# Two centring instructions of VectorE change their place in a graph layer with a residual norm

## The chip, the cores and the metric

The kernel runs on one core of a Trainium2 chip. The metric is the time of one execution on the device in microseconds (us), lower is better; the time before is the median of three runs. Engines are called as in the profile: PE (TensorE), DVE (VectorE), ACT (ScalarE), POOL (GpSimd), SP (SyncE, which only issues DMAs here).

## The reference

`x` has 50,000 rows (nodes) of 64 numbers; there are 25,000 edges with `src`, `dst` (sorted), a type out of 10 and 64 attributes.

```
t_r = x[src] @ W[type];  h_r = x[dst] @ W[type]
att = sum(t_r * tanh(h_r + edge_attr))
a   = softmax of att over the edges of one dst
h   = sum over the edges of one dst of x[src] * a
out = leaky((x + h) @ W1.T) + leaky((x * h) @ W2.T)
y   = layernorm(x + out)
```

Nodes without an edge have h = 0; for them, and at first for all, only the dense part x + leaky(x @ W1.T) and its norm count.

## The kernel before, in words

**Dense part.** The 50,000 rows are 49 dense tiles of 1024 rows (128 partitions x 8 rows of 64 numbers = 128 x 512). Each is loaded by SP, transposed and multiplied by PE, then on DVE added (`dense_add`, L974), summed per row (`dense_total`, L979), centred (`dense_centre`, L984: row sum x -1/64 + row, all in SBUF); ACT squares it (`dense_square`, L684); DVE sums the squares (`dense_sum`, L989); ACT takes the root (L730), DVE its inverse (L996), ACT scales each row (`dense_norm`, L691) and SP stores it (L311).

**Edge part.** The edges lie as 128 partitions x 196 columns; a block is 8 columns, 25 blocks. POOL gathers the rows of x for both ends of a column by an indirect DMA (L441), 384 in all; some columns are fetched row by row by SP (L377). DVE multiplies the transposed rows by ten type masks (`mask(s, 0..9)`, L912, reading PSUM), PE multiplies with the ten weights, ACT takes tanh, DVE the product (L919). One step later come the scores: the running maximum (`score_max`, L928), `differences` (L936, L937), `restarts` (L942), ACT's exponentials and weighting, and eight running sums `sum_one` (L954, 128 x 64). Two steps later the ending block: `pair` (L1004, L1005: h + x and h * x), PE's products, `leaky` (L1011), `final_add` (L1016), `final_add_x` (L1021). Three steps later, for block l: `final_sum` (L1026), `final_centre` (L1032), ACT's `final_square` (L736), `final_squares` (L1039), and ACT's `final_out` (L743). POOL then scatters the finished rows column by column over the dense result by an indirect DMA (L465), 196 in all.

**Order.** Each engine has its own queue, written out by hand as a loop over steps s = -1 to 28. In step s DVE handles masks of block s, scores and sums of e = s - 1, the ending of f = s - 2, the norm of l = s - 3, and dense tiles D0, D1, D2 = 3s+3, 3s+4, 3s+5; DP = 3s + 2 is the last dense tile of the step before. Dense tiles end with step 15. Engines wait on semaphores only; an instruction that follows one of its own engine waits only where a semaphore is named.

POOL's whole work is one queue: all gathers, then a wait for all dense stores, then all scatters. Before most of them it waits for a mark of PE's progress (`pace`), before a block's gathers for a free buffer (13 deep), before a block's scatters for ACT's scaled rows:

```
for s in range(NS):
    gather(s)
for k in range(RO):
    pool.wait_ge(o_stored[k], o_need(k))
...
def scatter(s):
    pool.wait_ge(fmul_done, s + 1)
    for j in range(cols(s)):
        pace(G_MOVES[NS] + c, s)
        pool.indirect_dma_start(...)
```

The last issue of POOL (L482) is a single row block for groups of edges that cross partitions.

Of the kernel before, what the change touches and what calls it, by code (L numbers as in the profile page):

```python
# [34 lines left out]
def wait(eng, sem, value):  # L35

    if value > 0:
        eng.wait_ge(sem, value)


def gnn_resnorm(nc, x, src, dst, eattr, etype, relw, resw, resw2, out):
# [14 lines left out]
    def cols(s):  # L56
        return min(COLS, T - s * COLS)

    def groups(s):
        return cols(s) // QUAD  # L60
# [7 lines left out]
    def tiles(s):  # L68
        return [d for d in range(3 * s + 3, 3 * s + 6) if 0 <= d < ND]
# [26 lines left out]
    with ExitStack() as ctx:  # L96
# [317 lines left out]
        def _(pool):  # L414
# [12 lines left out]
            def pace(n, scattered_blocks):  # L427
                step_end = ends[min(NS - 1, RW + 4 + scattered_blocks)]
                need = [k for k, (_, _, work) in enumerate(marks) if work <= min(n * PACE - LEAD if n < G_MOVES[NS] else n * PACE_OUT - LEAD_OUT, step_end)]
                if need and need[-1] > at[0]:  # L430
                    at[0] = need[-1]
                    pool.wait_ge(marks[at[0]][0], marks[at[0]][1])
# [395 lines left out]
        def _(v):  # L828
# [77 lines left out]
            def mask(s, r):  # L906
                n = cols(s) * P
                if r == 0:
                    v.wait_ge(xT_done, s + 1)
                    v.wait_ge(typ_in[s % RT], turn(s, RT) * DMA)  # L910
                wait(v, quad_done, s * R + r + 1 - RM)
                v.scalar_tensor_tensor(xm[:, (s * R + r) % RM, 0:n], typ[:, s % RT, 0:n], float(r), xT_ps[:, 0:n],  # L912
                                       ALU.is_equal, ALU.mult).then_inc(masked, 1)
# [7 lines left out]
            def score_max(e):  # L921
                c, n = e * COLS, cols(e)
                b = (e % 2) * COLS
                v.wait_ge(att_done, e + 1)
                if e == 0:
                    v.wait_ge(setup_d, 3)
                wait(v, max_done, e)
                v.tensor_tensor_scan(m_all[:, c + 1:c + 1 + n], start[:, c:c + n], s_ps[:, b:b + n],  # L928
                                     m_all[:, c:c + 1], ALU.add, ALU.max).then_inc(max_done, 1)
# [14 lines left out]
            def sum_one(e, j):  # L944
                if j >= cols(e):
                    return
                c = e * COLS + j
                v.wait_ge(wx_done, G_BEFORE[e] + j // QUAD + 1)
                wait(v, chain_done, c)
                if j == 0 and e >= RS:  # L950
                    v.wait_ge(h_done, G_BEFORE[e - RS + 1])
                    v.wait_ge(hist_stored[e % RS], e // RS * DMA)
                old = es[:, e % RS, j - 1, :] if j else es[:, (e - 1) % RS, COLS - 1, :]
                v.scalar_tensor_tensor(es[:, e % RS, j, :], old, wd[:, e % 2, 1, j:j + 1], wx[:, j, :],  # L954
                                       ALU.mult, ALU.add).then_inc(chain_done, 1)
# [25 lines left out]
            def dense_centre(d):  # L981
                v.wait_ge(zsum_done, d + 1)
                z = zd[:, d % RZ, :].rearrange("p (j f) -> p j f", f=D)
                v.scalar_tensor_tensor(z, zsd[:, :].unsqueeze(2).to_broadcast([P, DR, D]), -1.0 / D, z, ALU.mult, ALU.add).then_inc(zmid_done, 1)  # L984
# [13 lines left out]
            def pair(f):  # L998
                n = cols(f)
                xd = xsd[:, f % RX, 0:n, 1, :]  # L1000
                v.wait_ge(h_done, G_BEFORE[f + 1])
                if f > 0:
                    v.wait_ge(tr_in, TR_PAIR[f - 1, groups(f - 1) - 1] + 1)
                v.tensor_tensor(uw[:, 0:n, 0, :], h_t[:, 0:n, :], xd, ALU.add)  # L1004
                v.tensor_tensor(uw[:, 0:n, 1, :], h_t[:, 0:n, :], xd, ALU.mult).then_inc(uw_done, 1)  # L1005
# [22 lines left out]
            def final_centre(f):  # L1028
                n = cols(f)
                v.wait_ge(fsum_done, f + 1)  # L1030
                wait(v, fmul_done, f - 1)
                v.scalar_tensor_tensor(zcf[:, f % 2, 0:n, :], zs[:, 0:n].unsqueeze(2).to_broadcast([P, n, D]), -1.0 / D,  # L1032
                                       zf[:, 0:n, :], ALU.mult, ALU.add).then_inc(fsub_done, 1)
# [8 lines left out]
            for s in range(-1, LAST + 1):  # L1042
                main, e, f, l = 0 <= s < NS, s - 1, s - 2, s - 3
                D0, D1, D2 = (n if n in tiles(s) else None for n in (3 * s + 3, 3 * s + 4, 3 * s + 5))
                DP = 3 * s + 2 if 3 * s + 2 in tiles(s - 1) else None
                on, ending, late = 0 <= e < NS, 0 <= f < NS, 0 <= l < NS
# [7 lines left out]
                    mask(s, 1)  # L1054
                if on:
                    score_max(e)
                if DP is not None:
                    dense_centre(DP)
                if main:
                    mask(s, 2)  # L1060
                if on:
# [4 lines left out]
                    restarts(e)  # L1066
                if ending:
                    pair(f)
                if main:
                    mask(s, 4)  # L1070
                if main:
# [25 lines left out]
                    mask(s, 8)  # L1097
                if D0 is not None:
                    dense_centre(D0)
                if on:  # L1100
                    sum_one(e, 6)
                    sum_one(e, 7)
                if late:
                    final_centre(l)
                if main:
                    mask(s, 9)
                if D1 is not None:
# [105 lines left out]
```

## Time and profile before

| what | us |
|---|---|
| median of three runs (772.3 to 774.19) | 772.67 |
| the profiled execution | 767.71 |
| its span, first to last instruction | 765.7 |
| POOL's gathers (L441), 384 | 377.8 busy |
| POOL's scatters (L465), 196 | 201.6 busy |
| DVE busy | 634.9 |

Busy time is the time in which an engine had an instruction of the program in work. In a timeline a row is start, duration, engine, line, operation, output and inputs, shapes, count; instructions of one line that follow each other are merged into one row. Idle time of the engine ahead of an instruction stands in brackets, with what ended it; "issue" means that no wait shows. Consecutive DVE instructions overlap a little in the records: each starts some 0.08 us before the end of the one ahead.

### The profile page before, as it was taken

To read this page: it belongs to the slowest core of one execution; us is meant where nothing else is said; L and a number is where in the kernel's file an instruction comes from. 1 tells how busy PE (TensorE), PEld (TensorE's weight loads), DVE (VectorE), ACT (ScalarE), POOL (GpSimd) and SP (SyncE) were. 2 spreads that over 40 slices of the span, in tenths; PEclk is the share of its full clock that TensorE was granted. 3 is DMA by queue.
4 is the path that set the end of the run, shared out by engine and by line. 5 is a ranking of instruction groups with operands and counts; after the bars stand their busy time and mean duration, and the time that the engine had idled before them with its cause. 6 is when DMAs were issued, how large, how long until landed. Compare 5 with 4: busy or idle time off the path is not lost. (4 is left out here: it accounts for less than half of the span.)

```text
span 765.7 us, 14665 instructions
## 1 busy us (share of the span) xinstructions
PE 552.6 (72%) x3780; PEld 291.9 (38%) x3780; DVE 634.9 (83%) x1115; ACT 498.1 (65%) x1474; POOL 582.5 (76%) x590
## 2 busy tenths in 40 slices
PE   1887888888788788788888887888888778532000
PEld 0552454445345345345345343433333333321000
DVE  1689999999999999999999999999999989742010
ACT  0366768679779779779779777765665446755040
POOL 6777777777777777777777777777777777777776
PEclk9999999999999999999999999999999989855555
DMA  5463434434434434433433332322112221000000
GB/s 132 111 185 82 124 98 134 123 83 151 123 91 140 125 98 133 128 109 120 137 107 111 107 107 69 107 73 74 37 56 73 73 79 48 30 26 17 19 18 16
DMA packets 49457, 70.41 MB, mean 92 GB/s; under 512 B 17450, under 2 KB 20966, under 8 KB 49374
## 3 DMA queue, kind: packets, MB, share of 16 engines
q1 hardware_dynamic: 30750, 52.33, 21.1%
q0 software_dynamic: 18624, 17.16, 10.5%
q8 instruction: 30, 0.49, 0.3%
q14 instruction: 53, 0.43, 0.2%
HBM read 45.61 MB, written 25.78 MB: 93 GB/s over the span
## 5 line engine op out<-in xcount | busy, mean ns | idle before, releaser
L441 POOL DMA_INDIRECT xsd<-in_x,ends_i x384 | 377.8, 984 | 117.9 <-issue 110.7
L543 PE MATMUL t_ps<-xm,w_rel 64*64 64x512 f32 (+1 forms) x1000 | 269.4, 620 | 38.3 <-DVE xm L912 35.6
L912 DVE SCALAR_TENSOR_TENSOR xm<-typ,xT_ps 128x1024 f32<-128x1024 f32 (+1 forms) x250 | 291.8, 1184 | 2.7 <-issue 2.7
L545 PE MATMUL h_ps<-xm,w_rel 64*64 64x512 f32 (+1 forms) x1000 | 269.4, 620 | 0.0
L465 POOL DMA_INDIRECT out<-out_r,row_i x196 | 201.6, 1029 | 60.0 <-issue 57.2
L560 PE MATMUL y_ps<-bd_cat,dT 128*128 128x256 f32 x392 | 97.9, 394 | 19.7 <-DVE zd L974 17.5
L691 ACT ACTIVATE o_t<-zd,rstd 128x64 f32<-128x64 f32 x392 | 98.8, 339 | 15.3 <-DVE rstd L996 15.3
L543 PEld LDWEIGHTS t_ps<-xm,w_rel 64*64 64x64 f32 x1000 | 52.7, 134 | 142.0 <-DVE xm L912 107.0
L578 PE MATMUL s_ps<-bd_both,uwT 128*128 128x128 f32 x392 | 72.6, 310 | 39.9 <-issue 39.1
L578 PEld LDWEIGHTS s_ps<-bd_both,uwT 128*128 128x128 f32 x392 | 54.3, 200 | 115.9 <-issue 96.1
L560 PEld LDWEIGHTS y_ps<-bd_cat,dT 128*128 128x128 f32 x392 | 72.7, 195 | 33.1 <-issue 14.6
L698 ACT ACTIVATE wd<-delta 128x16 f32<-128x16 f32 (+1 forms) x25 | 5.4, 216 | 97.2 <-DVE delta L942 55.4
L954 DVE SCALAR_TENSOR_TENSOR es<-es,wd,wx 128x64 f32<-128x64 f32 x196 | 55.3, 282 | 11.6 <-ACT wx L704 0.6
L568 PE MATMUL tr_ps<-ident,uw 128*128 128x128 f32 x196 | 32.9, 292 | 27.5 <-ACT uwT L718 15.5
L545 PEld LDWEIGHTS h_ps<-xm,w_rel 64*64 64x64 f32 x1000 | 52.7, 134 | 0.0
L704 ACT ACTIVATE wx<-xsd,wd 128x64 f32<-128x64 f32 x196 | 52.1, 337 | 0.8
L723 ACT COPY l<-s_ps 128x256 f32<-128x256 f32 x98 | 35.3, 360 | 24.1 <-PE s_ps L578 24.1
L711 ACT ACTIVATE h_t<-es,rs 128x64 f32<-128x64 f32 x196 | 49.4, 337 | 0.0
L743 ACT ACTIVATE out_r<-zcf,rstd 128x64 f32<-128x64 f32 x196 | 49.1, 333 | 0.1
L568 PEld LDWEIGHTS tr_ps<-ident,uw 128*128 128x128 f32 x196 | 21.4, 145 | 67.2 <-issue 36.0
L974 DVE TENSOR_TENSOR zd<-rd,y_ps 128x512 f32<-128x512 f32 x49 | 33.3, 679 | 9.6 <-ACT rd L677 9.0
L736 ACT ACTIVATE sqf<-zcf 128x512 f32<-128x512 f32 (+1 forms) x25 | 15.6, 622 | 34.4 <-DVE zcf L1032 33.6
(143 smaller groups left out, 753.8 us busy)
## 6 DMA issues: line engine op xcount, KB each, us to landing
xsd<-in_x SPq DMA_DIRECT2D x1024, 0.2 KB
x_in<-in_x SPq DMA_DIRECT2D x48, 256.0 KB
typ<-typ_d SPq DMA_DIRECT2D x24, 512.0 KB
out<-o_t SPq DMA_DIRECT2D x48, 256.0 KB
xsd<-in_x,ends_i POOLq DMA_INDIRECT x384
hist<-es SPq DMA_DIRECT2D x24, 256.0 KB, 2.0
ea<-in_edge_attr SPq DMA_DIRECT2D x24, 224.0 KB
out<-out_r,row_i POOLq DMA_INDIRECT x196, 2.2
```

Of the source, the lines that this page charges most:

```text
L441: pool.indirect_dma_start(xsd[:, s % RX, j, side, :], None, x[:, :], bass.IndirectOffsetOnAxis(ap=ends_i[:, side, c:c + 1], axis=0),).then ...
L465: pool.indirect_dma_start(out[:, :], bass.IndirectOffsetOnAxis(ap=row_i[:, c:c + 1], axis=0), out_r[:, s % RW, j, :], None, bounds_check=t ...
L543: pe.matmul(t_ps[h * D:(h + 1) * D, 0:n], w_rel[0:D, r, :], xm[0:D, b, h * n:(h + 1) * n], start=(r == 0), stop=(r == R - 1), skip_group_c ...
L545: mm = pe.matmul(h_ps[(1 - h) * D:(2 - h) * D, 0:n], w_rel[D:P, r, :], xm[D:P, b, (1 - h) * n:(2 - h) * n], start=False, stop=(r == R - 1) ...
L560: mm = pe.matmul(y_ps[:, j * 2 * P:(j + 1) * 2 * P], dT[:, d % 2, j * P:(j + 1) * P], bd_cat.rearrange("p k f -> p (k f)"), start=True, st ...
L568: mm = pe.transpose(tr_ps[:, j * P:(j + 1) * P], uw[:, g * QUAD + j, :, :].rearrange("p k f -> p (k f)"), ident[:, :])
L578: mm = pe.matmul(s_ps[:, YQ + j * P:YQ + (j + 1) * P], uwT[:, q // 2, k * P:(k + 1) * P], bd_both[:, :], start=True, stop=True)
L691: ins = act.activation(o_t[:, d % RO, j * D:(j + 1) * D], zd[:, d % RZ, j * D:(j + 1) * D], ACT.Copy, scale=rstd[:, s % 2, d % 3, j:j + 1])
L704: ins = act.activation(wx[:, j, :], xsd[:, e % RX, j, 0, :], ACT.Copy, scale=wd[:, e % 2, 0, j:j + 1])
L711: ins = act.activation(h_t[:, j, :], es[:, f % RS, j, :], ACT.Copy, scale=rs[:, f % 2, j:j + 1])
L912: v.scalar_tensor_tensor(xm[:, (s * R + r) % RM, 0:n], typ[:, s % RT, 0:n], float(r), xT_ps[:, 0:n], ALU.is_equal, ALU.mult).then_inc(mask ...
L954: v.scalar_tensor_tensor(es[:, e % RS, j, :], old, wd[:, e % 2, 1, j:j + 1], wx[:, j, :], ALU.mult, ALU.add).then_inc(chain_done, 1)
```

## The change

DVE's queue is reordered at two places; no instruction is added, removed or altered, and the other engines' queues are the same. In a step the centring of tile DP stood behind `score_max` and ahead of mask 2; it now stands behind `pair` (L1004, L1005) and ahead of mask 4. `final_centre` of block l stood behind `sum_one` 6 and 7 and ahead of mask 9; it now stands behind the centring of D0 and ahead of sums 6 and 7.

```
                 if on:
                     score_max(e)
-                if DP is not None:
-                    dense_centre(DP)
                 if main:
                     mask(s, 2)
...
                     restarts(e)
                 if ending:
                     pair(f)
+                if DP is not None:
+                    dense_centre(DP)
                 if main:
                     mask(s, 4)
...
                     mask(s, 8)
                 if D0 is not None:
                     dense_centre(D0)
+                if late:
+                    final_centre(l)
                 if on:
                     sum_one(e, 6)
                     sum_one(e, 7)
-                if late:
-                    final_centre(l)
                 if main:
                     mask(s, 9)
```

## Rows read from the trace of the kernel before

**Rows 1.** The page: busy us of each engine, share of the span, instructions.

```profile
PE 552.6 (72%) x3780; PEld 291.9 (38%) x3780; DVE 634.9 (83%) x1115; ACT 498.1 (65%) x1474; POOL 582.5 (76%) x590
```

**Rows 2.** POOL's waits: us in total, times, longest us.

```profile
POOL xsd L441 <- issue: 110.7, 363, 0.3
```

**Rows 3.** Groups of POOL's instructions: busy us, mean ns | idle before.

```profile
L441 POOL DMA_INDIRECT xsd<-in_x,ends_i x384 | 377.8, 984 | 117.9 <-issue 110.7 <-PE h_ps L545 2.7 <-PE s_ps L578 1.5
L465 POOL DMA_INDIRECT out<-out_r,row_i x196 | 201.6, 1029 | 60.0 <-issue 57.2 <-PE h_ps L545 1.8 <-PE s_ps L578 0.6
```

**Rows 4.** Timeline of POOL, last block and last issue.

```profile
756.21 0.97 POOL L465 DMA_INDIRECT out<-out_r,row_i  x1 [0.30 <-issue]
...
761.32 0.97 POOL L482 DMA_INDIRECT out<-out_fix,fix_i  x1 [0.30 <-issue]
```

**Rows 5.** Timeline of ACT, the last finished rows.

```profile
737.25 1.05 ACT L743 ACTIVATE out_r<-zcf,rstd 128x64 f32<-128x64 f32 x4
```

**Rows 6.** Timeline of POOL in the gather phase.

```profile
303.01 1.24 POOL L441 DMA_INDIRECT xsd<-in_x,ends_i  x1 [0.30 <-issue]
...
313.31 1.46 POOL L441 DMA_INDIRECT xsd<-in_x,ends_i  x1 [0.30 <-issue]
...
325.06 0.94 POOL L441 DMA_INDIRECT xsd<-in_x,ends_i  x1 [0.30 <-issue]
...
479.76 2.04 POOL L441 DMA_INDIRECT xsd<-in_x,ends_i  x1 [0.30 <-issue]
```

**Rows 7.** Timeline of DVE over the same stretch.

```profile
302.26 1.17 DVE L1011 SCALAR_TENSOR_TENSOR l<-l 128x1024 f32<-128x1024 f32 x1
...
307.78 2.34 DVE L912 SCALAR_TENSOR_TENSOR xm<-typ,xT_ps 128x1024 f32<-128x1024 f32 x2
...
310.18 0.68 DVE L984 SCALAR_TENSOR_TENSOR zd<-zsd,zd 128x512 f32<-128x512 f32 x1
...
313.27 0.68 DVE L1004 TENSOR_TENSOR uw<-h_t,xsd 128x512 f32<-128x512 f32 x1
313.87 0.68 DVE L1005 TENSOR_TENSOR uw<-h_t,xsd 128x512 f32<-128x512 f32 x1
...
324.49 0.68 DVE L984 SCALAR_TENSOR_TENSOR zd<-zsd,zd 128x512 f32<-128x512 f32 x1
325.08 0.68 DVE L954 SCALAR_TENSOR_TENSOR es<-es,wd,wx 128x64 f32<-128x64 f32 x2
...
336.09 2.34 DVE L912 SCALAR_TENSOR_TENSOR xm<-typ,xT_ps 128x1024 f32<-128x1024 f32 x2
...
479.70 0.68 DVE L1004 TENSOR_TENSOR uw<-h_t,xsd 128x512 f32<-128x512 f32 x1
```

**Rows 8.** Timeline of ACT: its square of the step's tile DP.

```profile
314.60 0.61 ACT L684 ACTIVATE sqd<-zd 128x512 f32<-128x512 f32 x1
```

**Rows 9.** Timeline of POOL in the scatter phase.

```profile
511.56 1.46 POOL L465 DMA_INDIRECT out<-out_r,row_i  x1 [0.30 <-issue]
...
517.15 1.50 POOL L465 DMA_INDIRECT out<-out_r,row_i  x1 [0.30 <-issue]
...
536.00 1.87 POOL L465 DMA_INDIRECT out<-out_r,row_i  x1 [0.31 <-issue]
```

**Rows 10.** Timeline of DVE in the scatter phase.

```profile
510.90 0.66 DVE L954 SCALAR_TENSOR_TENSOR es<-es,wd,wx 128x64 f32<-128x64 f32 x2
511.48 0.69 DVE L1032 SCALAR_TENSOR_TENSOR zcf<-zs,zf 128x512 f32<-128x512 f32 x1
...
514.64 1.22 DVE L1011 SCALAR_TENSOR_TENSOR l<-l 128x1024 f32<-128x1024 f32 x1 [0.37 <-ACT l L723]
...
517.12 0.67 DVE L1021 TENSOR_TENSOR zf<-zf,xsd 128x512 f32<-128x512 f32 x1
```

**Rows 11.** Timeline of POOL: the first scatter.

```profile
498.65 1.00 POOL L465 DMA_INDIRECT out<-out_r,row_i  x1 [0.54 <-issue]
```

**Rows 12.** Timeline of SP: the last dense tile's store.

```profile
495.25 0.73 SPq L311 DMA_DIRECT2D out<-o_t  x2
```

More of the change, by code:

```diff
@@ L1056, in _ @@
                     score_max(e)
-                if DP is not None:
-                    dense_centre(DP)
                 if main:
@@ L1068, in _ @@
                     pair(f)
+                if DP is not None:
+                    dense_centre(DP)
                 if main:
@@ L1099, in _ @@
                     dense_centre(D0)
+                if late:
+                    final_centre(l)
                 if on:
@@ L1102, in _ @@
                     sum_one(e, 7)
-                if late:
-                    final_centre(l)
                 if main:
```

## The prediction

> **What bounds the kernel now.** I read the busy times first. DVE is busy for 83% of the span, POOL for 76%, PE for 72% [rows 1], so the share alone points at DVE. It misleads here. The second view is POOL's waits: POOL's idle time before its 580 indirect DMAs is nearly all "issue", 0.3 us at most before a gather [rows 2] and the same before scatters but for one 0.54 us [rows 11]. An engine that never waits is the bound. The groups of POOL's instructions give the sum: 384 gathers of 984 ns and 117.9 us between them, 196 scatters of 1029 ns and 60.0 us between them [rows 3]: 377.8 + 117.9 + 201.6 + 60.0 = 757.3 us. The last issue ends at 761.32 + 0.97 = 762.3 us [rows 4]; the 5.0 us that the sum lacks are the setup ahead of the first gather and two single issues. What follows is the last landing, to 765.7 us. The data are ready long before: the last finished rows are scaled at 737.25 to 738.3 us and their first scatter starts at 756.21 us [rows 4, 5], 17.9 us later. No other engine has work on the output after that.
>
> So an edit of DVE's order counts only by what it does to POOL. There are two ways: DVE's marks come so late that POOL must wait, or DVE slows POOL's issues.
>
> The second way is visible. Most gathers last 0.94 us, but in every step one lasts 1.24 and one 1.46 us [rows 6]. Lay DVE's timeline beside them [rows 7]. The gather at 303.01 starts inside L1011 (302.26 to 303.43) and ends at 304.25, 0.82 us behind L1011's end. The one at 313.31 starts 0.04 us after L1004 did (313.27 to 313.95) and ends at 314.77, again 0.82 us behind. The scatter at 511.56 starts inside L1032 (511.48 to 512.17), lasts 1.46 in place of 0.97, and ends 0.85 us behind it; the one at 517.15 does the same with L1021 [rows 9, 10]. I call such an issue caught. What catches is a long DVE instruction with two SBUF inputs: L984, L1004, L1005, L1011, L1016, L1021, L1032. The ten masks of a step (one input in PSUM) and L954 (64 columns) catch nothing. An issue that starts less than 0.13 us before the DVE instruction's end, or just before its start, goes free: the gather at 325.06 starts inside L984's last 0.11 us and lasts 0.94 [rows 6, 7].
>
> This also ties POOL to DVE while dense tiles last. A DVE step takes 336.09 - 307.78 = 28.31 us [rows 7]; POOL makes 22 issues in it, 22 x 1.25 = 27.5 us free, and the two catches (0.30 + 0.51 = 0.81 us) fill the rest. A POOL that ran ahead would be caught longer, and so held to DVE's step. The pattern stands from about 142 to 455 us, eleven times.
>
> **Part one: the last dense tile's centring (L984) goes from behind the running maximum to behind the pair, in steps 0 to 15.** Nothing is added or removed: one DVE instruction of 0.68 us, with the next one starting 0.60 us behind its start (as from 313.27 to 313.87), changes place [rows 7]. Masks 2 and 3, the differences and the pair come 0.60 us earlier, mask 4 and all behind it stay. Who waits? ACT squares that tile at 314.60 [rows 8]; in the new order the centring ends at about 313.87 + 0.68 = 314.55, so the square moves by nothing. If that cover went, ACT's queue behind it (the eight scalings of finished rows, then the pair's copy) would slip by up to the 0.6 us moved. The earlier restarts and pair can only help ACT's weights and PE. The square's sum on DVE comes two masks later, over 2 us. Cost on DVE: 0.
>
> For POOL, the slot from 313.87 to 314.55 that was L1005's is now L984's, the slot that was L1004's (313.27) is L1005's, and L1004 lies one slot earlier, where no issue starts (the gather before starts 1.25 us ahead of 313.31, at 312.06, the new L1004 at 312.67). So the same gather is caught by an instruction of the same length: 0. The old place of L984 (310.18) caught nothing in these steps, so nothing is gained there.
>
> The Trainium skill speaks against this part: its page "SBUF — State Buffer", section "SBUF: two separate sides", says that DVE and GpSimd share a port pair as an exclusive lock, against a GpSimd operation that reads SBUF whenever DVE has two SBUF inputs, and that the loser blocks fully. By that rule three such instructions in a row are a longer barrier than two; the rows agree that the loser blocks, and what it makes of the time is the third rival.
>
> **Part two: centring of finished rows (L1032) goes ahead of running sums 6 and 7, in steps 3 to 27.** Again one instruction of 0.60 us moves. Sums 6 and 7 come 0.60 us later; behind them are the store of the history on SP (its buffer comes round only four steps later) and the normaliser, whose place is behind mask 9 and stays. ACT's square of these rows may start earlier, but in the dense steps ACT is busy with the tile's own square until then; in the later steps pair outputs bound by PE decide, so DVE's step does not shorten. Cost on DVE: 0; bounds 0.2 us either way per run.
>
> In the gather phase the new L1032 starts at about 325.08, a few hundredths from the gather at 325.06. A catch needs DVE to be first by about 0.03 us (the narrowest seen is L1021's 517.12 against 517.15). I take: not caught. If caught, it costs 0.68 - 0.13 = 0.55 us once, not per step, since POOL then meets L1016 and the new L984 in place of L1011 and L1005, with again some 0.8 us per step.
>
> In the scatter phase the move has an effect. At 511.56 the old L1032 caught a scatter for 0.48 us; the new one occupies 510.90 to 511.58 [rows 10], and that scatter goes free. The same stands twice more (about 554 and 596 us): 3 x 0.48 = 1.44 us. Further on: the issues come 0.48 us earlier, one starts at 515.39 inside L1011 (514.64 to 515.86) and is caught for 0.34, the next at 517.01 is ahead of L1021's 517.12 and is spared 0.52. Sum of the first passage: -0.48 + 0.34 - 0.52 = -0.66 us. Two DVE steps on, the shift also turns the long catch at 536.00 (1.87 us, 0.90 over [rows 9]) into one of 0.3. Three passages together give at most -3 us. But after about 610 us the masks thin out and the catches are irregular; the longest, L1011 at full length, costs 1.22 - 0.12 = 1.1 us. An issue stream shifted by 1 to 3 us meets other instructions there, and with starts laid against the rows two catches take 1.8 us back. I take -1.2 us; the ends are -3.0 and, if more is taken back than was gained, +1.5.
>
> **Sum** against the profiled execution: 0 + 0 - 1.2, so a span of 764.5 us, from 765.7. Its own time, 767.71, lies 5.0 us below the median of the three runs, 772.67; I carry the difference over: 772.67 - 1.2 = 771.5 us. What can be told from no change is 0.3%, 2.3 us.
>
> **Rivals.**
> (a) Much more is gained in the scatter phase: all three passages hold and nothing is taken back, -3.0 us, 769.7. For it: the three passages are alike to 0.01 us. Against: L1021 caught by 0.03 us only, so in other runs that catch may not exist, and the gain neither.
> (b) POOL is caught by the new L1032 once, and the scatter phase falls badly: +0.6 + 1.5 = +2.1, 774.8.
> (c) Slower: the longer barrier. At 479.76 a gather was caught by L1004 (479.70) and held through L1005 as well: 2.04 us, 1.10 over [rows 6, 7]. With three in a row such a gather would be held some 0.6 us more. If that became the rule, the 0.30 at L1011 would vanish but 0.3 us per step stay, over 14 steps +4.2 us: 776.9. It decides from 0.16 us per step. Against: of the steady steps not one shows it; POOL gets in between two DVE instructions nearly always.
> (d) DVE's dense step itself changes by some 0.1 us, as ACT or PE get their work sooner; POOL is tied to that step, so 15 x 0.1 = 1.5 us either way: 770.0 to 773.0 together with the forecast, still within 0.3% or at its edge.
> (e) The first scatter waits for the last dense tile's store, issued at 495.25 [rows 12], 2.9 us ahead of the last gather's end at 498.11; the scatter's idle time is 0.54 in place of 0.30 us [rows 11]. SP is busy issuing single rows before it, so the edit moves it little: up to 0.5 us if late.
>
> **Chances.** The forecast with (d) and (e), within 0.3%: 0.68. (a) and its like, faster by over 2.3 us: 0.20. (c), and the worst of (b): 0.12. The range reaches to (a) and to (b): 769.3 to 774.7.
>
> **What would show it.** POOL idle before issues still at most 0.3 us; DVE's step in the dense phase still 28.31 us; the gather phase ends near 498.1 us, with L1005 in L1004's place as the catcher at 0.5 us; no scatter caught by L1032 between 500 and 610 us; ACT's square of the last dense tile unmoved. The prediction is wrong if gathers of 1.5 us appear at L1032, if issues of 2 us appear at the pair, or if POOL shows waits on PE's marks.

## The result and the profile after

The changed kernel takes 766.85 us (median of 4 runs, 766.31 to 767.59) against 772.88 us before (4 runs): ratio 0.992, 95% interval 0.9893 to 0.9947, so 6.0 us or 0.8% faster. The forecast was 771.5 us, within 0.3%; the range ended at 769.3. On a second chip the ratio was 0.9955 (0.9936 to 0.9974), 3.8 us.

The profiled execution of the changed kernel has a span of 764.9 us, only 0.8 us less than the 765.7 of before. One profile of each kernel therefore doesn't carry the explanation; the experiments below do.

What the two profiles do give is the time by phase. POOL's 85th and last scatters, before and then after:

```profile
612.67 0.97 POOL L465 DMA_INDIRECT out<-out_r,row_i  x1 [0.30 <-issue]
...
760.04 0.97 POOL L465 DMA_INDIRECT out<-out_r,row_i  x1 [0.31 <-issue]
```

```profile
609.72 0.97 POOL L465 DMA_INDIRECT out<-out_r,row_i  x1 [0.30 <-PE h_ps L545]
...
759.15 0.97 POOL L465 DMA_INDIRECT out<-out_r,row_i  x1 [0.30 <-issue]
```

The last gather ends at 498.11 us before and at 498.53 after. The first 84 scatters (from the first one's start to the 85th's) take 114.0 us before and 110.9 after; the other 112, to the end of the last, take 148.3 and 150.4. So in this pair the scatter phase gains 3.1 us and gives 2.1 back, close to the 3.0 and 1.8 of the prediction, and the gather phase is no shorter.

POOL's waits and groups after, in the columns of [rows 2, 3]:

```profile
POOL xsd L441 <- issue: 108.6, 356, 0.3
...
POOL out L465 <- issue: 55.5, 182, 0.3
```

```profile
L441 POOL DMA_INDIRECT xsd<-in_x,ends_i x384 | 378.2, 985 | 118.0 <-issue 108.6 <-PE h_ps L545 5.5 <-PE y_ps L560 1.2
L465 POOL DMA_INDIRECT out<-out_r,row_i x196 | 200.6, 1023 | 59.7 <-issue 55.5 <-PE h_ps L545 3.4 <-PE s_ps L578 0.9
```

POOL is still the engine that hardly ever waits: 378.2 + 118.0 + 200.6 + 59.7 = 756.5 us of its own work and issue time.

DVE's timeline in the dense phase, and POOL's beside it (for [rows 7] and [rows 6]):

```profile
278.92 1.21 DVE L912 SCALAR_TENSOR_TENSOR xm<-typ,xT_ps 128x1024 f32<-128x1024 f32 x1
...
307.11 2.34 DVE L912 SCALAR_TENSOR_TENSOR xm<-typ,xT_ps 128x1024 f32<-128x1024 f32 x2
...
311.99 0.69 DVE L1004 TENSOR_TENSOR uw<-h_t,xsd 128x512 f32<-128x512 f32 x1
312.59 0.69 DVE L1005 TENSOR_TENSOR uw<-h_t,xsd 128x512 f32<-128x512 f32 x1
313.19 0.69 DVE L984 SCALAR_TENSOR_TENSOR zd<-zsd,zd 128x512 f32<-128x512 f32 x1
...
324.41 0.71 DVE L1032 SCALAR_TENSOR_TENSOR zcf<-zs,zf 128x512 f32<-128x512 f32 x1
```

```profile
312.63 1.47 POOL L441 DMA_INDIRECT xsd<-in_x,ends_i  x1 [0.30 <-issue]
...
324.39 0.95 POOL L441 DMA_INDIRECT xsd<-in_x,ends_i  x1 [0.30 <-issue]
```

The catcher of the long gather is now L1005: it starts 0.04 us ahead of the gather at 312.63, which lasts 0.52 us too long, as L1004 did before. The new L1032 starts 0.02 us behind the gather at 324.39 and catches nothing. But the step is 307.11 - 278.92 = 28.19 us, where it was 28.31.

Three of this profile's dense steps are longer again, by 0.35 us each. In them DVE waits at L919, the product that needs ACT's tanh (L667):

```profile
331.95 0.69 DVE L919 TENSOR_TENSOR prod<-t_ps,g_t 128x512 f32<-128x512 f32 x1 [0.26 <-ACT g_t L667]
```

The other profile of the changed kernel has three such waits as well, that of part one alone has two of 0.12 and 0.17 us, and no profile of a kernel without part one has any. What makes ACT late there is not shown.

ACT's timeline at the two squares. First after, then before (rows that were not shown ahead of the prediction):

```profile
313.92 0.63 ACT L684 ACTIVATE sqd<-zd 128x512 f32<-128x512 f32 x1 [0.49 <-DVE zd L984]
...
325.03 0.63 ACT L684 ACTIVATE sqd<-zd 128x512 f32<-128x512 f32 x1
325.56 0.62 ACT L736 ACTIVATE sqf<-zcf 128x512 f32<-128x512 f32 x1
326.08 0.58 ACT L677 ACTIVATE rd<-y_ps 128x512 f32<-128x512 f32 x1
```

```profile
325.70 0.63 ACT L684 ACTIVATE sqd<-zd 128x512 f32<-128x512 f32 x1
326.39 0.63 ACT L736 ACTIVATE sqf<-zcf 128x512 f32<-128x512 f32 x1
326.93 0.58 ACT L677 ACTIVATE rd<-y_ps 128x512 f32<-128x512 f32 x1
```

The square of DP lies 313.92 - 307.11 = 6.81 us into the step; before it was 314.60 - 307.78 = 6.82. It didn't move. At the other place, from L684's start to L677's it is 1.23 us before and 1.05 after. Before, ACT waited there for the final centring for a few hundredths of a microsecond, and the relu (L677) came late for DVE's add of tile D1.

POOL's timeline in the scatter phase after (for [rows 9, 11]):

```profile
498.83 1.00 POOL L465 DMA_INDIRECT out<-out_r,row_i  x1 [0.30 <-issue]
...
510.71 0.97 POOL L465 DMA_INDIRECT out<-out_r,row_i  x1 [0.30 <-issue]
...
514.54 1.34 POOL L465 DMA_INDIRECT out<-out_r,row_i  x1 [0.30 <-PE h_ps L545]
516.18 0.97 POOL L465 DMA_INDIRECT out<-out_r,row_i  x1 [0.30 <-issue]
```

In this phase no scatter is caught by L1032; the one at 514.54 is caught by L1011 for 0.36 us, and L1021 is passed.

### The profile page after: what moved, and what is told of

The parts are those of the page before. It is cut to its first block and busy times, and to the rows that moved or that the text cites. A ratio compares the mean times of both kernels' runs of the same rounds, so it can differ in the third digit from the quotient of the medians.

```text
span 764.9 us, 14665 instructions
## 1 busy us (share of the span) xinstructions
PE 556.2 (73%) x3780; PEld 293.9 (38%) x3780; DVE 634.8 (83%) x1115; ACT 499.1 (65%) x1474; POOL 581.8 (76%) x590
## 5 line engine op out<-in xcount | busy, mean ns | idle before, releaser
L441 POOL DMA_INDIRECT xsd<-in_x,ends_i x384 | 378.2, 985 | 118.0 <-issue 108.6
L465 POOL DMA_INDIRECT out<-out_r,row_i x196 | 200.6, 1023 | 59.7 <-issue 55.5
L954 DVE SCALAR_TENSOR_TENSOR es<-es,wd,wx 128x64 f32<-128x64 f32 x196 | 55.7, 284 | 11.7 <-ACT wx L704 0.6
L684 ACT ACTIVATE sqd<-zd 128x512 f32<-128x512 f32 x49 | 30.9, 631 | 12.7 <-DVE zd L984 12.6
```

The source lines that it names most:

```text
L441: pool.indirect_dma_start(xsd[:, s % RX, j, side, :], None, x[:, :], bass.IndirectOffsetOnAxis(ap=ends_i[:, side, c:c + 1], axis=0),).then ...
L465: pool.indirect_dma_start(out[:, :], bass.IndirectOffsetOnAxis(ap=row_i[:, c:c + 1], axis=0), out_r[:, s % RW, j, :], None, bounds_check=t ...
```

## The experiments

In each, the ratio is to runs of the kernel before on the same chip. It is not exactly the quotient of the two medians, so microseconds by the ratio and by the medians can differ by up to 1 us. The chips differ: the kernel before has medians of 767.4 (first four kernels), 769.4 (second four) and 768.2 us (third four), so only ratios are compared between them.

### The kernel before against itself

> The kernel before, unchanged, timed against itself. Theory 1 (catches on POOL's issues: which issues are caught depends on how the issue stream lies against DVE's instructions, and the kernel before can lie in more than one way): ratio 1.000 and a time of 772 to 774 us, while its profiled execution may fall at 767 to 768 or at 772 to 774 us; in the latter POOL shows 5 us more time in its issues than the 25.8 us above their free lengths (0.946 us a gather, 0.975 us a scatter) that the profile of before shows, and still no idle time over 0.55 us. Theory 2 (POOL waits in those executions for PE's marks): a slow execution would show POOL idle for more than 0.5 us at some issues, in sum 5 us.

Measured: ratio 0.9984 (0.9974 to 0.9994), 766.5 us; runs of 765.65 to 769.62. The interval leaves out 1 though the kernels are identical, so a difference under 0.2% means little. Its profiled execution, 769.62 us, is the longest of its ten, with this first scatter:

```profile
500.46 1.00 POOL L465 DMA_INDIRECT out<-out_r,row_i  x1 [1.75 <-DMA out<-o_t]
```

DVE's first mask started at 33.64 us in it, at 31.82 in the profile of before, and this delay reached the end: POOL waited for the last dense tile's store. Theory 1's claim, that a longer execution has more time in the issues, is hardly what this one shows: above the free lengths of 0.946 and 0.975 us the gathers and scatters have 25.9 us, in the profile of before 25.0 (not the 25.8 of the expectation). Theory 2's claim, idle time at PE's marks, doesn't appear at all. The 2.1 us by which its span is longer are mostly that late start. The 772 to 774 us of the first chip did not come back on it.

### Each part alone, and both

```
# part one alone
-                if DP is not None:
-                    dense_centre(DP)      (behind score_max)
+                if DP is not None:
+                    dense_centre(DP)      (behind pair)
# part two alone
+                if late:
+                    final_centre(l)
                 if on:
                     sum_one(e, 6)
                     sum_one(e, 7)
-                if late:
-                    final_centre(l)
```

> Part one alone: DP's centring behind the pair, final centring where it was. Theory 1a (the gain of 6 us is made in the dense phase, where part one works on all 16 steps): 766 to 768 us, -5 to -7. Theory 1b (the gain is made by the final centring's new place): 772 to 774 us, no change. My prediction's sum said 0 for this part.

> Part two alone: the final centring ahead of running sums 6 and 7, DP's centring where it was. Theory 1a: 771 to 773 us, 0 to -1.5. Theory 1b: 766 to 768 us, -5 to -7. My prediction's sum said -1.2 for this part.

> Both parts, the changed kernel again on the same chip as its parts: 766 to 768 us by either theory; if it comes out at 772 to 774 here, the difference is between chips and not between kernels.

| kernel | median us | ratio | 95% interval |
|---|---|---|---|
| part one | 766.88 | 0.9993 | 0.9974 to 1.0013 |
| part two | 763.68 | 0.9946 | 0.9924 to 0.9968 |
| both | 763.57 | 0.9955 | 0.9936 to 0.9974 |

The whole gain is part two's. Part one gives nothing that can be told from zero, as the sum had it; its interval spans 3 us. The size is 0.45 to 0.54% here, less than on the first chip.

### Part two by phase, and the last dense store

```
# dense steps only: the new place if s <= 15, else the old one
+                if late and s <= 15:
+                    final_centre(l)
                 (sums 6 and 7)
+                if late and s > 15:
+                    final_centre(l)
# late steps only: the two conditions exchanged
# store: in SP's queue
+                if s == 16:
+                    for n in tiles(s - 1)[0:2]:
+                        store_o(n)
                 rows_at((s - 1) * PER_STEP + 2)
                 (the stores behind it, now only if s is not 16)
```

> Part two in steps 3 to 15 only. Theory L (the last dense tile's store sets when the scatters begin: in the three profiles without part two the first scatter starts 0.90 us behind the store's landing, and part two shortens DVE's dense step from 28.31 to 28.19 us, so that store comes earlier): -1.5 to -2.5 us against before, and the first scatter not later than 0.55 us behind the last gather. Theory C (fewer issues caught by L1032 in the scatter phase): no change, within 0.5 us.

> Part two in steps 16 to 27 only. Theory L: no change, within 0.5 us; DVE's dense step stays 28.31 us. Theory C: -1.3 to -3 us, with under 1 us of POOL's scatters caught by L1032 in place of 2.1 to 3.7. Both together would give -1.5 to -2.5 here and the same at the dense steps.

> The kernel before, with one thing moved in SP's queue: in step 16 the last dense tile's store stands ahead of 16 single-row loads instead of behind them, so it is issued some 3.5 us earlier. Theory L: -0.5 to -2 us (the profiles of before and of its repeat show 0.24 and 1.45 us of wait at the first scatter beyond the usual 0.30), and the first scatter 0.3 us behind the last gather. Theory C: no change.

> Part two (all steps) with that store moved as well. Theory L: the landing is then out of the way, and what is left of part two's gain is what the gather and scatter phases give: 0 to -1 us beyond part two alone (763.7 us where before is 767.4). Theory C: the same as part two alone, within 0.5 us.

| kernel | median us | ratio | 95% interval |
|---|---|---|---|
| dense steps only | 767.47 | 0.9978 | 0.9970 to 0.9987 |
| late steps only | 765.38 | 0.9955 | 0.9942 to 0.9967 |
| store alone | 768.85 | 1.0000 | 0.9992 to 1.0009 |
| part two and store | 763.85 | 0.9930 | 0.9919 to 0.9942 |

Two gains stand beside each other: 0.22% (1.7 us) from the dense steps and 0.45% (3.5 us) from the late ones; their sum, 0.67%, is close to the 0.70% of part two and the store together. The first of them is barely above the 0.16% by which the kernel differed from itself; what supports it is DVE's shorter step. Neither theory alone was right. Theory L as to the store fell: with the store out of the way the time is the same within 0.1%. What that store can cost shows in an execution in which DVE starts late. The profile of the store alone has such a start too (first mask at 33.67 us, in the kernel against itself at 33.64), and its first scatter starts at 499.17 us where the other's waited until 500.46.

For the late steps two profiles of this batch can be laid side by side, since one of the kernels (store alone) runs like before. POOL's timeline with the centring at the old place (store alone; L469 is its scatter):

```profile
513.55 1.45 POOL L469 DMA_INDIRECT out<-out_r,row_i  x1 [0.30 <-issue]
...
519.16 1.48 POOL L469 DMA_INDIRECT out<-out_r,row_i  x1 [0.30 <-issue]
...
538.00 1.86 POOL L469 DMA_INDIRECT out<-out_r,row_i  x1 [0.31 <-issue]
```

POOL's timeline with it at the new place in the late steps, and DVE's:

```profile
511.76 0.97 POOL L465 DMA_INDIRECT out<-out_r,row_i  x1 [0.30 <-issue]
...
515.59 1.32 POOL L465 DMA_INDIRECT out<-out_r,row_i  x1 [0.30 <-issue]
517.22 0.98 POOL L465 DMA_INDIRECT out<-out_r,row_i  x1 [0.30 <-issue]
...
536.75 1.32 POOL L465 DMA_INDIRECT out<-out_r,row_i  x1 [0.30 <-issue]
```

```profile
511.10 0.68 DVE L1032 SCALAR_TENSOR_TENSOR zcf<-zs,zf 128x512 f32<-128x512 f32 x1
...
514.84 1.22 DVE L1011 SCALAR_TENSOR_TENSOR l<-l 128x1024 f32<-128x1024 f32 x1 [0.33 <-ACT l L723]
...
517.31 0.68 DVE L1021 TENSOR_TENSOR zf<-zf,xsd 128x512 f32<-128x512 f32 x1
```

At the old place the profile repeats [rows 9] to 0.02 us a catch: 0.48, 0.51, 0.89. At the new one the scatter at 511.76 starts 0.02 us before L1032's end and goes free, the one at 515.59 is caught by L1011 for 0.35, the one at 517.22 is 0.09 us ahead of L1021, and in place of 0.89 stands 0.35. That is the first passage as the prediction laid it out (0.34 at L1011, ahead of L1021), and then the second and third. The first 84 scatters take 114.43 us (499.17 to 613.60) at the old place and 110.69 (498.80 to 609.49) at the new one: -3.7 us. The 112 from there to the end take 148.25 and 148.79 us: +0.5 us back. Counted in issues, POOL makes 15 and 16 in turn in DVE's late steps of 21.15 us at the old place, and 16 in each at the new one. One issue more in every second step, 1.27 us each, is the same gain.

This pair is not the whole record. The old place has a second pattern. In the profile of "dense steps only" the late steps are those of before, and yet it shows this in every step:

```profile
509.58 1.46 POOL L465 DMA_INDIRECT out<-out_r,row_i  x1 [0.30 <-issue]
...
530.80 1.46 POOL L465 DMA_INDIRECT out<-out_r,row_i  x1 [0.30 <-issue]
```

L1032 catches a scatter each time for 0.48 us, but the catches at L1021 and the long one at L1011 are missing, POOL makes 16 issues a step, and the first 84 scatters take 111.4 us. All profiles on chips where POOL is the bound, but for two with one more instruction in the late steps, by the place of the final centring there:

| place, profiles | first 84, us | other 112, us |
|---|---|---|
| old: before, before against itself, store alone | 113.9 to 114.4 | 148.3 to 148.7 |
| old: part one | 112.3 | 148.7 |
| old: dense steps only; ACT's order (below) | 111.4; 111.6 | 147.8; 148.3 |
| old: longer dense step (below) | 112.8 | 147.4 |
| new: after, part two, both, late steps only, part two and store | 110.6 to 111.4 | 148.7 to 150.4 |

So the new place avoids the slow pattern in all five of its profiles, and the old one sometimes does so too, by how POOL happens to enter the phase. The profiles of "dense steps only" and of ACT's order are each the shortest execution of their kernel (763.33 us where the next is 766.95; 763.73 where the median is 766.59), so the fast pattern is probably not their usual one; how often an unprofiled execution falls into it is not on record. What is given back behind the 84th scatter is 0.5 us only in the pair above. Over these profiles it lies between nothing and 3 us.

### Catches by themselves

```
+                if 17 <= s <= 23:
+                    v.tensor_tensor(free buffer 128x1024, typ[...], typ[...], ALU.mult)
                 if main:
                     mask(s, 6)
# the other kernel: second input xT_ps (PSUM) in place of typ
```

> The kernel before with one more DVE instruction in each of steps 17 to 23, ahead of mask 6: a product of 128x1024 with both inputs in SBUF, written to a buffer that is free by then (its result is not used). DVE gets 7 x 1.1 = 8 us more work, which POOL's lead of 14 us and more covers. Theory C (POOL's issue is held while a long DVE instruction reads two SBUF inputs): a scatter that starts anywhere in the first 1.05 us of it is held to its end, on average 7 x 0.43 = 3 us; expected +1 to +5 us. Rival R (what counts is when DVE's work ends, or nothing): the same as the next run, within 1 us.

> The same extra product with one input in PSUM, of the same size and at the same place. Theory C: no scatter is held by it; the time moves by no more than a shift of the other catches makes, -1.5 to +1.5 us, and is clearly below the run with two SBUF inputs. Rival R: both runs move alike.

Two SBUF inputs: 771.28 us, ratio 1.0049 (1.0029 to 1.0068). One: 770.27 us, ratio 1.0027 (1.0008 to 1.0046). The two intervals overlap, so the times alone don't decide. The rows do. DVE and POOL with two SBUF inputs:

```profile
549.31 1.22 DVE L1081 TENSOR_TENSOR x_in<-typ 128x1024 f32<-128x1024 f32 x1
```

```profile
550.25 1.13 POOL L465 DMA_INDIRECT out<-out_r,row_i  x1 [0.30 <-issue]
```

and with one:

```profile
548.92 1.22 DVE L1081 TENSOR_TENSOR x_in<-typ,xT_ps 128x1024 f32<-128x1024 f32 x1
```

```profile
549.85 0.97 POOL L465 DMA_INDIRECT out<-out_r,row_i  x1 [0.30 <-issue]
```

DVE's instruction has the same length, and the scatter starts 0.94 and 0.93 us into it. With two SBUF inputs the scatter lasts 1.13 us, with one 0.97. This is so in all seven steps (1.11 to 1.13 against 0.97): DVE's instruction with two SBUF inputs holds the issue, the one with an input in PSUM doesn't. 7 x 0.15 = 1.0 us is also the difference of the medians, but that is a coincidence: in the two profiles the first 84 scatters, with five of the seven holds, take 115.13 and 115.10 us, so the holds were made good elsewhere. I had expected 3 us; POOL's issues happened to meet only the last 0.28 us of the instruction each time. That both kernels are slower than before by 2 us at least was not foreseen beyond my 1.5 us. In their profiles about that much is there before the first extra instruction (at 505.47 and 505.08 us) has run. The first scatter, with two SBUF inputs and with one, where it was 498.65 before:

```profile
500.89 1.00 POOL L465 DMA_INDIRECT out<-out_r,row_i  x1 [0.30 <-issue]
```

```profile
500.50 1.00 POOL L465 DMA_INDIRECT out<-out_r,row_i  x1 [0.30 <-issue]
```

Each has one gather in the dense phase that was held through both L1004 and L1005 (at 199.34 and 227.62 us, 2.05 us long), and from that step on POOL is one issue behind. The edit adds nothing to those steps; it acts from step 17. So the times of these two kernels say little of the extra instruction, and the rows carry the reading alone.

### What ties POOL to DVE in the dense phase, and where the 0.12 us are from

```
# longer dense step, in steps 3 to 15, ahead of mask 6
+                    v.tensor_tensor(extra[:, 0:256], typ[...0:256], xT_ps[:, 0:256], ALU.mult)
# ACT's order alone, DVE unchanged
+                if D1 is not None:
+                    dense_relu(D1)
                 if 0 <= l < NS:
                     final_square(l)
-                if D1 is not None:
-                    dense_relu(D1)
```

> The kernel before with one more short DVE instruction (128x256, one input in PSUM, result not used) in each of steps 3 to 15: DVE's dense step grows by about 0.3 us, 13 x 0.3 = 3.9 us. Theory T (POOL's gathers are tied to DVE's step by the catches): most of it appears in the time, +2.5 to +4.5 us, and the last gather ends that much later. Rival F (POOL issues at its own pace): 0 to +0.5 us.

> The kernel before with ACT's queue changed at one place and DVE's not at all: the relu of dense tile D1 goes ahead of the square of the finished rows. If part two shortened the dense step because DVE's add of D1 (L974) waited for that relu, and the relu stood behind a square that waited for the final centring, this run too has a dense step of 28.19 us or less in place of 28.31 and gains -1 to -2 us; the scatter phase is as before. If the shorter step had another cause, the step stays 28.31 us and the time the same.

The longer step: DVE's dense step becomes 337.48 - 308.86 = 28.62 us. Its first masks in two dense steps, and POOL's last gather:

```profile
308.86 2.34 DVE L913 SCALAR_TENSOR_TENSOR xm<-typ,xT_ps 128x1024 f32<-128x1024 f32 x2
...
337.48 2.34 DVE L913 SCALAR_TENSOR_TENSOR xm<-typ,xT_ps 128x1024 f32<-128x1024 f32 x2
```

```profile
501.27 0.94 POOL L442 DMA_INDIRECT xsd<-in_x,ends_i  x1 [0.30 <-issue]
```

The last gather ends at 502.2 us where it was 498.1, 4.1 us for 13 x 0.31 = 4.0 us of DVE. POOL makes 22 issues in each of these steps, as it did at 28.31 us. POOL's idle time before each issue stays 0.30: it is held in its issues alone, and tied to DVE's step. First scatter of that kernel (L466 in it), for [rows 11]:

```profile
502.51 1.00 POOL L466 DMA_INDIRECT out<-out_r,row_i  x1 [0.30 <-issue]
```

The time grew less, ratio 1.0021 (0.9998 to 1.0045), 770.06 us: the scatter phase of its profile is 2.2 us shorter than that of before. The stretch is tied; what it hands on to the next is not kept whole.

ACT's order alone: 766.59 us, ratio 0.9967 (0.9943 to 0.9991), -1.6 us by the medians and -2.5 by the ratio. ACT's timeline of it:

```profile
324.76 0.63 ACT L684 ACTIVATE sqd<-zd 128x512 f32<-128x512 f32 x1
325.29 0.58 ACT L677 ACTIVATE rd<-y_ps 128x512 f32<-128x512 f32 x1
325.76 0.62 ACT L736 ACTIVATE sqf<-zcf 128x512 f32<-128x512 f32 x1
```

DVE's dense step is 306.84 - 278.69 = 28.15 us:

```profile
278.69 2.34 DVE L912 SCALAR_TENSOR_TENSOR xm<-typ,xT_ps 128x1024 f32<-128x1024 f32 x2
...
306.84 2.34 DVE L912 SCALAR_TENSOR_TENSOR xm<-typ,xT_ps 128x1024 f32<-128x1024 f32 x2
```

With DVE's queue untouched the dense step shrinks as under part two. So the 0.12 us were the relu's lateness: DVE's add of D1 waited for it behind mask 9. The last gather of this profile ends at 496.4 us, 1.7 earlier than before. The expectation that the scatter phase is as before did not hold in it: it lies in the fast pattern (first 84 in 111.6 us), so not all of this kernel's gain need be the dense step's.

### Earlier still, and the fastest version: on chips where POOL is not the bound

```
# late steps: the centring ahead of sums 4 and 5, or behind them
+                if late and s > 15:
+                    final_centre(l)
                 if on:
                     sum_one(e, 4)
                     sum_one(e, 5)
# third kernel: part two in all steps and ACT's order as above
```

> In steps 16 to 27 only, the final centring stands ahead of sums 4 and 5 (2.5 us earlier than in the kernel before, 1.9 us earlier than in part two). Laid against the rows of before, the scatter at 509.00 would start 0.06 us inside it (508.94 to 509.6) and be held for 0.48 us, just as the one at 511.56 is in the kernel before, at every second step. Theory C (where the centring meets POOL's starts): first 84 scatters 113 to 114.5 us as in the profile of before (114.0), total within 1 us of before. Theory E (the earlier the centring, the sooner ACT, PE and DVE go on): at least the gain of part two in the late steps, -3 us or more.

> The same, but behind sums 4 and 5, ahead of the inverse roots: 0.6 us later than the run above, 1.9 us earlier than before. The scatter at 510.28 starts 0.1 us behind its end (509.5 to 510.2) and goes free. Theory C: first 84 scatters 110.5 to 111.5 us, total -2 to -4 us, as with part two in the late steps. Theory E: the same as the run above, within 0.5 us.

> Part two in all steps, with ACT's relu of D1 ahead of the square of finished rows as well: a candidate for the fastest. The dense step should be 28.15 to 28.19 us, the first 84 scatters 110.5 to 111.5 us; total -4 to -5.5 us against before. If the relu's new place adds nothing to part two, it equals part two alone (0.9946 on another chip).

> The same kernel as h1, on another chip; on the first one every kernel took 915 us with POOL waiting for over 100 us, which says nothing of catches. In steps 16 to 27 the final centring stands ahead of sums 4 and 5, where by the rows of before it meets a scatter's start at every second step. Theory C: first 84 scatters 113 to 114.5 us, total within 1 us of before. Theory E (earlier is better): -3 us or more.

> The same kernel as h2, on another chip: the centring behind sums 4 and 5. Theory C: first 84 scatters 110.5 to 111.5 us, total -2 to -4 us. Theory E: as the run above, within 0.5 us.

> The same kernel as h3, on another chip: part two in all steps and ACT's relu of D1 ahead of the square. Dense step 28.15 to 28.19 us, first 84 scatters 110.5 to 111.5 us, total -4 to -5.5 us against before.

Both times, on two chips, the kernel before itself took 915 to 916 us. The ratios: ahead of sums 4 and 5 0.9994 and 1.0006, behind them 1.0000 and 0.9987, part two with ACT's order 0.9997 and 0.9994, all with intervals that hold 1. The first of these on the second chip, POOL's waits ("remote" is a wait that the profile can't tie to an instruction of this core's queues):

```profile
POOL xsd L441 <- remote: 59.1, 41, 3.7
POOL xsd L441 <- PE h_ps L545: 27.7, 27, 1.9
...
POOL out L465 <- DMA out<-o_t: 12.6, 1, 12.6
```

The mean granted clock of TensorE is 0.845 there, 0.91 to 0.93 in the profiles on the other chips, and the dense steps take 31 to 37 us. POOL waits for marks of PE and, for 12.6 us, for the last dense store. It is likely that what a catch costs is then taken from a wait; no run was made to show it. So the question behind these runs stays open in its direct form, and whether part two with ACT's order is the fastest version wasn't measured where it could show. The lowest ratios measured are 0.992, of the changed kernel on the first chip, and 0.993, of part two with the store moved on another.

## Why the prediction was wrong

**The bound: right.** POOL's queue sets the end; it is idle 0.3 us before its issues in the profile after, and the rows show no other way for DVE's edits to act. The list of what catches has one line too many: no issue started inside L1016 in any of the fourteen profiles in which POOL is the bound, so whether it catches is not shown. The tie to DVE's step in the dense phase was right too and was shown by the longer step.

**Part one, 0: right within the noise.** Alone it gives 0.9993 (0.9974 to 1.0013). In the profile after, L1005 took L1004's place as the catcher and the square of DP lies at 6.81 us in the step against 6.82. "Cost on DVE: 0" is not quite what the rows show: the waits at L919 make DVE's thirteen dense steps 1.0 us longer with both parts (368.5 us) than with part two alone (367.5), and no time on record shows that. The barrier of rival (c) exists but is rare: in the profile after one gather of the dense steps was held from L1005 through L984.

```profile
170.77 2.07 POOL L441 DMA_INDIRECT xsd<-in_x,ends_i  x1 [0.30 <-issue]
```

It cost POOL one issue's place in that step (21 in place of 22), and POOL stayed behind. In the other profile of the same kernel, which has the waits at L919 but no such hold, the gather phase ends at 497.36 us in place of 498.53; the hold is what kept the profile after from ending it earlier than before. Part one is not needed for such a hold: the two kernels with the extra product had one each through L1004 and L1005, three such holds in the steady dense steps of fourteen profiles.

**Part two, dense steps, "Cost on DVE: 0": this step failed.** I wrote that in the dense steps ACT is busy with the tile's own square until the final centring is there. It was busy until a few hundredths before it, and behind that wait stood the relu for which DVE's add of D1 waited. The step shrank by 0.12 us, some 13 times, and POOL is tied to it. That makes 1.6 us; measured were 1.7 (0.9978), 1.6 to 2.5 us with ACT's order alone. Rival (d) had this mechanism and the price, 1.5 us, but it was counted as inside the forecast.

**Part two, late steps, "-1.2 us": the mechanism was right, this term was mis-sized.** 1.2 us was forecast and 3.5 us (0.9955) measured. Of its two sizes, the gain of the passages was put at 3.0 us at most, though the prediction's own rows add up to 0.66 + 0.60 = 1.26 us a passage and 3.8 for three; measured were 3.7 in the pair of the experiments and 3.1 in the pair of the result. The part that the irregular end takes back was put at 1.8 and measured 0.5 in the one pair and 2.1 in the other. It was the weak term: it rested on two catches, laid behind the last rows that repeat. So the pair that the forecast was worked out from came out at about its net size, -1 us in the scatter phase, and the timed runs did not: they gained some 2 us more. Which of the two patterns each execution falls into could make that difference; that is argued, not shown. Rival (a) was this case, with its 3.0 us, and had 0.20.

**The base of the sum.** The 5.0 us between the profiled execution and the median of before were carried over unchanged. The changed kernel has none of it: its profiled execution, 766.97 us, lies at its median. Why before took 5 us more on that chip is not shown.

**The sum.** The two terms make 5.2 us, 0.67%. On the chip of the result the kernel was 6.0 us faster, on the next 3.8; the interval of the one is 0.9893 to 0.9947 and of the other 0.9936 to 0.9974, which both hold 0.994. What else differed on the first chip, where before took 772 to 774 us in runs and 767.71 in the profiled execution, stays open. So does whether the late gain is all from catches: the profile pair of the experiments shows 3.7 us less in the first 84 scatters with fewer and shorter catches, and the run made to separate place from earliness fell on chips that can't tell.

## What to carry to other kernels

When one engine issues back to back without waiting, look at the length of its single issues, not at the waits, and lay the long ones beside the other engines' rows. Moving one instruction by 0.6 us can be worth 0.5% there with no work saved. Price a reordering in the busiest loop also by waits of a few hundredths of a microsecond: repeated in every step on an engine that is always busy, they count whole. And one profile fixes a pattern only where it repeats, and even then it may be one of two that the same queues can fall into: see where a profile's time lies among the other runs before taking sizes from it, and take a second one.

## What the runs showed of the hardware

- An indirect DMA issue of POOL (0.94 us for a gather, 0.97 for a scatter) that starts while a long DVE instruction reads two SBUF inputs ends 0.82 to 0.85 us behind that instruction's end; with one input in PSUM the same instruction holds nothing. Over the fourteen profiles in which POOL is the bound, some 2,200 issues started while a mask (one input in PSUM) alone was in work with over 0.13 us of it to go, and none was held by more than 0.03 us. The Trainium skill, page "SBUF — State Buffer", section "Who interferes with whom", says that DVE with two SBUF inputs contends with a GpSimd instruction that reads SBUF. The rows agree for these issues: with two SBUF inputs 1.11 to 1.13 us, with one 0.97.
- DVE's 128x64 instruction with two SBUF inputs and a per-partition scalar (L954) held hardly any: of the issues that started in those profiles while it alone was in work none ended more than 0.07 us late. It lasts only 0.28 us.
- Two engines that meet in this way fall into step: POOL made 22 issues per DVE step at 28.31 us and again at 28.62. In late steps of 21.15 us it made 31 in two steps before and 32 after. A gather held through two instructions (2.05 to 2.07 us) put it one issue behind, and it stayed there.
- The same program took 767 to 769 us on three chips, 773 on the one of the result, and 915 us on two others; the mean granted clock was about 0.92 on the three and 0.84 on the two.
